# Moving the D*u term of a state-space scan from VectorE to ScalarE and TensorE, in twenty of its groups

## The chip, the cores and the metric

The kernel runs on one core of one Trainium2 chip. Its time is the device time of one execution in microseconds (us); of several runs the median is given. TensorE is called PE here, VectorE DVE, ScalarE ACT, GpSimd POOL and SyncE SP, as in the profile.

## The reference

Two layers, each a Mamba mixer and a mixture-of-experts feed-forward block, on an input of 4 x 512 rows of 512 features. What matters here is the mixer. For each of 2 layers, 4 batches and 512 channels e it computes, over l = 0..511,

```python
delta = softplus(dt_proj @ dt_low + dt_b)              # [b, e, l]
state = state * exp(delta * A[e, n]) + delta * u * Bm[n]   # n = 0..15
y[e]  = sum over n of state[n] * Cm[n]
y     = y + D[e] * u                                   # the term in question
y     = y * silu(z)
x     = x + transpose(y)
```

`u` is the activated output of a short convolution, which depends on the context input alone, so both layers' scans can be run one behind the other. The feed-forward block of layer 0 (shared expert and eight routed ones) follows from its mixer, that of layer 1 from the second mixer.

## The kernel before, in words

**Stages.** A first stretch projects and convolves for all eight pairs of layer and batch (`projections`). Then `scan_stage` runs 32 groups g = 0..31: layer 0's four batches of four blocks of 128 channels, then layer 1's. A group has 16 steps, one for each state i; one tile is 128 channels x 512 positions, fp32. Beside the scans of groups 4 to 19 the shared expert of layer 0 is worked off in small pieces (class `Beside`, `Shared`), beside groups 21 to 31 the routed experts of layer 0. After all of it come the feed-forward blocks of layer 1 (`stage_ffn1`).

**Order.** Each engine's program is written out by hand: the loop `steps()` gives (g, i), and each engine issues its instructions for this step and then `side.step(...)`, its pieces of the other work. An engine runs its queue in order; semaphores join the engines. For step (g, i), s = 16 g + i:

- ACT, L570: H[i % 4] = exp(delta * A), into one of four PSUM banks. It waits until hC of step s - 4 is done, which read that bank.
- POOL, L608: dBu[i % 2] = du * B[i]. It waits until scan s - 2 is done.
- DVE, L661: the scan of step s, in place in H. Then, for the step before, L641: hC = H * C, into a ring of SBUF buffers. In groups 0 to 19 the ring has three buffers (`ring`), so hC(i) waits until PE has added up hC(i - 3).
- PE, L511 (`add_up`): YS += ident x hC, in PSUM bank 4. In the trace an fp32 matmul is two records, here and elsewhere.

From group 20 on (`paired`) POOL adds some of the hC in pairs (L620), and the ring has four buffers.

**The bank YS** is used in turn. The sum of group g - 1 is complete after its add_up 15. DVE's `dve_y` (L646) at step `y_at[g]` of group g (1 in groups up to 19, 2 after) computes Y = Y * D + YS; Y held u until then. Then PE's dt_proj for group g + 1 (L499, step `y_at[g] + 1`) writes its product over YS, once `y_done` allows. ACT reads that product in `prep(g + 1, 0)` (L548, L549), which releases `pre_read`; `prep` goes on in three more steps with softplus's exp, square, logarithm and a linear term (L552 to L560), one part behind each exp of steps `y_at[g] + 3` to `y_at[g] + 6`. PE's first add_up of group g (`add_up(g, 0)`, issued at step `y_at[g] + 2` with those of v = 1 and 2) waits for that `pre_read`. POOL finishes delta for group g + 1: `pool_poly` (L583) at step 9, `pool_delta` (L587) at 13, `pool_du` (L593) at 14; DVE picks at step 11 (L625).

**Side work on DVE that the prediction names:** L1001 (norm of a row tile), L986 and L990 (the two halves of the gated product, the second after PE's up-projection), L981 (adds the down-projection of a tile to X), L945 (gate). PE's products for it are L1024, its transposes L1020 and L1038; on ACT L1085 and L1097 read them.

Of the kernel before, what the change touches and what calls it, by code (L numbers as in the profile page):

```python
# [30 lines left out]
B, L, D = 4, 512, 512  # L31
# [71 lines left out]
def program(nc, x, ctxT, mix, moe0, moe1, out):  # L103
    ctx = ExitStack()
    with ctx:
# [288 lines left out]
        def scan_stage(side):  # L394
# [12 lines left out]
            hC = [wk(6), wk(7), wk(8), wk(19)]  # L407
            side.y_done = y_done

            def paired(g):  # L410

                return g >= side.PAIRS
# [82 lines left out]
            def tensor(pe):  # L495
                def dt_proj(g):
                    if g == GROUPS // 2:
                        pe.wait_ge(dt1_in, 32)
                    nc.tensor.matmul(YS[:, :], dtwT[:, g % NJ * P:(g % NJ + 1) * P], xds[:, g // NJ % B, :],  # L499
                                     start=True, stop=True).then_inc(dt_done, 1)  # L500

                def add_up(g, v):
                    u = units[g][v]
                    if v == 0:
                        at_least(pe, y_done, g)
                        pe.wait_ge(pre_read, min(g + 2, GROUPS))
                    if len(u) == 2:
                        pe.wait_ge(pool_added, pairs0[g] + pairs[g].index(u) + 1)
                    else:
                        pe.wait_ge(hC_done, g * NS + u[0] + 1)  # L510
                    nc.tensor.matmul(YS[:, :], ident[:, :], hC[ring(g * NS + u[0])], start=v == 0,  # L511
                                     stop=v == len(units[g]) - 1).then_inc(sum_done, 1)

                def first_step(pe):
                    free(pe, "pe")
                    dt_proj(0)

                proj_pe(pe, first_step)
                side.before("pe", pe)
                for g, i, vb, n in steps():  # L520
                    if g:
                        for v in range(len(units[g - 1])):
                            if when(g - 1, v) == NS + i:
                                add_up(g - 1, v)
                    if i == y_at[g] + 1 and g < GROUPS - 1:
                        at_least(pe, y_done, g)
                        pe.wait_ge(pre_read, g + 1)
                        dt_proj(g + 1)
                    if i >= y_at[g] + 2:
                        for v in range(len(units[g])):  # L530
                            if when(g, v) == i:
                                add_up(g, v)
                    side.step("pe", pe, vb, n)
                for v in range(len(units[-1])):
                    if when(GROUPS - 1, v) >= NS:
                        add_up(GROUPS - 1, v)
                side.after("pe", pe)

            def scalar(act):
                def prep(g, step):  # L540

                    j, k = g % NJ, g // NJ // B
                    if step == 0:
                        act.wait_ge(dt_done, g + 1)
                        at_least(act, dA_done, (g - 1) * NS)
                        at_least(act, dBu_done, (g - 1) * NS)
                        at_least(act, delta_done, g)
                        nc.scalar.activation(delta[j % 2], YS[:, :], ACT.Relu, bias=dtb[k][:, j:j + 1])  # L548
                        nc.scalar.activation(logp, YS[:, :], ACT.Abs, bias=dtb[k][:, j:j + 1]).then_inc(pre_read, 1)  # L549
                    if step == 1:  # L550
                        act.wait_ge(pre_read, g + 1)
                        nc.scalar.activation(expo, logp, ACT.Exp, scale=-1.0).then_inc(t_done, 1)  # L552
                    if step == 2:
                        act.wait_ge(t_done, g + 1)
                        nc.scalar.activation(poly, expo, ACT.Square, bias=pbias[:, 0:1], scale=3.0 ** -0.5).then_inc(sq_done, 1)
                        nc.scalar.activation(du[j % 2], expo, ACT.Relu, bias=pbias[:, 1:2], scale=-1.0)
                    if step == 3:
                        nc.scalar.activation(logp, expo, ACT.Ln, bias=1.0)
                        act.wait_ge(sq_done, g + 1)
                        nc.scalar.activation(poly, poly, ACT.Identity, bias=pbias[:, 2:3]).then_inc(sp_l, 1)  # L560

                proj_act(act, lambda step: prep(0, step))
                free(act, "act")
                side.before("act", act)
                for g, i, vb, n in steps():
                    s = g * NS + i
                    if i == 0:
                        act.wait_ge(delta_done, g + 1)
                    at_least(act, hC_done, s - 3)
                    nc.scalar.activation(H[i % 4][:, :], delta[g % 2], ACT.Exp,  # L570
                                         scale=An[vb // B][:, g % NJ, i:i + 1]).then_inc(dA_done, 1)
                    if y_at[g] + 3 <= i <= y_at[g] + 6 and g < GROUPS - 1:
                        prep(g + 1, i - y_at[g] - 3)
                    if g == 1 and i == 0:
                        free(act, "act gates")
                    if vb <= B:
                        side.gate("act", act, vb, *divmod(n, NS))
                    side.step("act", act, vb, n)
                side.after("act", act)
# [69 lines left out]
            def vector(dve):  # L649
                def first_step(dve):  # L650
                    dve.wait_ge(poly_done, 1)
                    dve_pick(0)

                proj_dve(dve, first_step)
                stats(dve)
                side.before("dve", dve)
                for g, i, vb, n in steps():
                    s = g * NS + i
                    dve.wait_ge(dA_done, s + 1)
                    dve.wait_ge(dBu_done, s + 1)  # L660
                    nc.vector.tensor_tensor_scan(H[i % 4][:, :], H[i % 4][:, :], dBu[i % 2], 0.0,  # L661
                                                 ALU.mult, ALU.add).then_inc(scan_done, 1)
                    if s:
                        dve_hC(dve, s - 1)
                    if i == y_at[g] and g:
                        dve_y(dve, g - 1)
                    if i == 11 and g < GROUPS - 1:
                        dve.wait_ge(poly_done, g + 2)
                        dve_pick(g + 1)
                    side.step("dve", dve, vb, n)  # L670
                dve_hC(dve, GROUPS * NS - 1)
                dve_y(dve, GROUPS - 1)
                side.after("dve", dve)
# [1138 lines left out]
```

## Time and profile before

| | |
|---|---|
| time, median of 3 runs | 2232.88 us (2231.13 to 2234.89) |
| the profiled execution | 2236.41 us, its span 2234.6 us |
| PE, busy | 1926.2 us, 86% of the span |
| DVE, busy | 1397.7 us, 63% |
| POOL, busy | 1052.3 us, 47% |
| ACT, busy | 850.3 us, 38% |
| scans, L661 | 512 of 1222 ns, from 138.0 us to 1357.0 us |
| L646 | 32 of 736 ns, from 172.8 us to 1361.4 us |

The profile is of one execution. Busy shares are means over stages that differ; which engine holds up a stage is read from the groups of that stage, and from what its busiest engine waited for. A wait is put down to what came last. Group 0 begins at 138.0 us, group 20 at 893.9 us, group 21 at 944.6 us. Within a timeline each line is one instruction or a few like ones, with its start, its length, and, in brackets, the time for which its engine stood idle before it and who ended that.

### The profile page before, as it was taken

How to read it: one execution, taken by the hardware profiler on the slowest of the kernel's cores; microseconds unless marked ns; L12 is line 12 of the kernel's file. 1: busy time of each engine (PE TensorE's matmuls, PEld its weight loads, DVE VectorE, ACT ScalarE, POOL GpSimd, SP SyncE). 2: the span in 40 equal slices, each digit the busy share in tenths (PEclk: the TensorE clock that was granted, in tenths of full speed). 3: DMA queues.
4: the chain of work that ended last, by engine and by line, in shares of the span. 5: the costliest groups of instructions: out<-in, count | busy, mean ns of one | idle time of the engine just before them, and what ended most of it. 6: DMA issues, size and time to landing. Idle time of an engine off the chain costs nothing. (4 is left out here: it accounts for less than half of the span.)

```text
span 2234.6 us, 18612 instructions
## 1 busy us (share of the span) xinstructions
PE 1926.2 (86%) x5075; PEld 879.4 (39%) x5075; DVE 1397.7 (63%) x1934; ACT 850.3 (38%) x1372; POOL 1052.3 (47%) x927
## 2 busy tenths in 40 slices
PE   8846778789688796589999994999999999999997
PEld 2212233334233242134444442545455555555553
DVE  6899999899888988688888886564311111111100
ACT  4746545546464543555555551111011111111111
POOL 0057776676676664887777774110651110111111
PEclk9968799899899997589999997899999999999999
DMA  5099300302302102558769666212656665666554
GB/s 195 27 308 193 151 10 10 150 15 78 120 13 118 48 10 113 183 217 319 267 222 354 235 217 215 82 57 86 208 166 181 177 185 165 171 185 173 183 160 149
DMA packets 102625, 341.62 MB, mean 153 GB/s; under 512 B 16944, under 2 KB 17968, under 8 KB 84480
## 3 DMA queue, kind: packets, MB, share of 16 engines
q1 hardware_dynamic: 89008, 312.09, 40.8%
q0 software_dynamic: 13520, 28.40, 5.7%
q8 instruction: 41, 0.67, 0.1%
q14 instruction: 56, 0.46, 0.1%
HBM read 276.53 MB, written 65.74 MB: 153 GB/s over the span
## 5 line engine op out<-in xcount | busy, mean ns | idle before, releaser
L608 POOL TENSOR_TENSOR work<-work,big 128x512 f32<-128x512 f32 x512 | 653.9, 1283 | 232.3 <-DVE bank L661 231.1
L511 PE MATMUL bank<-work,ident 128*128 128x512 f32 x928 | 533.3, 688 | 206.5 <-DVE work L641 156.6
L661 DVE TENSOR_TENSOR_SCAN bank<-bank,work 128x512 f32<-128x512 f32 x512 | 625.4, 1222 | 95.4 <-POOL work L608 50.9
L570 ACT ACTIVATE bank<-work,An 128x512 f32<-128x512 f32 x512 | 347.6, 690 | 324.8 <-DVE work L641 323.4
L511 PEld LDWEIGHTS bank<-work,ident 128*128 128x128 f32 x928 | 173.6, 210 | 509.8 <-DVE work L641 330.5
L641 DVE TENSOR_TENSOR work<-bank,big 128x512 f32<-128x512 f32 x512 | 344.8, 674 | 7.9 <-PE bank L511 7.5
L1723 PE MATMUL bank<-Y,big 128*128 128x512 f32 x528 | 259.2, 595 | 0.0
L1561 POOL DMA_INDIRECT out_rows<-Y,meta x39 | 61.3, 1571 | 375.8 <-ACT Y L1235 271.6
L1258 DVE SCALAR_TENSOR_TENSOR work<-work,bank 128x352 f32<-128x352 f32 (+1 forms) x62 | 35.9, 579 | 302.3 <-ACT work L1248 302.3
L1024 PE MATMUL bank<-W,work 128*128 128x512 f32 x384 | 191.6, 603 | 0.0
L1737 PE MATMUL bank<-big,W 128*128 128x512 f32 x352 | 168.3, 593 | 0.0
L1235 ACT ACTIVATE Y<-bank,meta 128x512 f32<-128x512 f32 x39 | 26.8, 687 | 293.7 <-PE bank L1213 278.8
L1723 PEld LDWEIGHTS bank<-Y,big 128*128 128x128 f32 x528 | 99.0, 191 | 82.6 <-issue 57.0
L1213 PE MATMUL bank<-work 128*128 128x512 f32 (+1 forms) x234 | 114.3, 600 | 4.1 <-DMA work<-down_last 4.1
L1202 PE MATMUL bank<-work 128*128 128x352 f32 x312 | 110.7, 460 | 1.3 <-DMA work<-up 1.3
L1263 DVE SCALAR_TENSOR_TENSOR work<-work,bank 128x352 f32<-128x352 f32 (+1 forms) x62 | 35.9, 579 | 120.9 <-PE bank L1202 120.9
L1674 ACT ACTIVATE work<-bank 128x512 f32<-128x512 f32 x44 | 26.2, 597 | 222.1 <-PE bank L1723 222.1
L1192 PE MATMUL bank<-work 128*128 128x352 f32 x312 | 105.9, 464 | 1.3 <-DMA work<-gate 1.3
L1024 PEld LDWEIGHTS bank<-W,work 128*128 128x128 f32 x384 | 72.6, 193 | 84.3 <-issue 84.2
L583 POOL TENSOR_TENSOR work<-work 128x512 f32<-128x512 f32 x32 | 40.6, 1268 | 115.0 <-ACT work L560 115.0
L1737 PEld LDWEIGHTS bank<-big,W 128*128 128x128 f32 x352 | 65.3, 190 | 58.6 <-issue 46.0
L1622 DVE SCALAR_TENSOR_TENSOR W<-work,bank 128x512 f32<-128x512 f32 x44 | 30.2, 686 | 92.7 <-PE bank L1723 92.4
(258 smaller groups left out, 2373.1 us busy)
## 6 DMA issues: line engine op xcount, KB each, us to landing
big<-bc_d SPq DMA_DIRECT2D x64, 1024.0 KB, 6.6
work<-gate SPq DMA_DIRECT2D x39, 704.0 KB, 4.2
work<-up SPq DMA_DIRECT2D x39, 704.0 KB, 4.2
W<-gate SPq DMA_DIRECT2D x23, 1024.0 KB, 4.9
W<-up SPq DMA_DIRECT2D x23, 1024.0 KB, 5.5
W<-down SPq DMA_DIRECT2D x23, 1024.0 KB, 5.3
work<-down SPq DMA_DIRECT2D x39, 512.0 KB, 3.7
work<-xs_d SPq DMA_DIRECT2D x62, 256.0 KB, 4.8
```

The lines of the kernel that those rows point to most:

```text
L511: nc.tensor.matmul(YS[:, :], ident[:, :], hC[ring(g * NS + u[0])], start=v == 0, stop=v == len(units[g]) - 1).then_inc(sum_done, 1)
L570: nc.scalar.activation(H[i % 4][:, :], delta[g % 2], ACT.Exp, scale=An[vb // B][:, g % NJ, i:i + 1]).then_inc(dA_done, 1)
L608: nc.gpsimd.tensor_tensor(dBu[i % 2], du[g % 2], Bb[:, i, :], ALU.mult).then_inc(dBu_done, 1)
L641: nc.vector.tensor_tensor(hC[ring(s)], H[i % 4][:, :], Cb[:, i, :], ALU.mult).then_inc(hC_done, 1)
L661: nc.vector.tensor_tensor_scan(H[i % 4][:, :], H[i % 4][:, :], dBu[i % 2], 0.0, ALU.mult, ALU.add).then_inc(scan_done, 1)
L1024: ins = nc.tensor.matmul(dst[:, :], at[:, c * P:(c + 1) * P], w[:, c, :], start=c == 0, stop=c == DK - 1)
L1192: ins = nc.tensor.matmul(self.G[:, 0:self.F], self.xT[q][:, c * P:(c + 1) * P], self.wg[:, c, :], start=c == 0, stop=c == DK - 1)
L1202: ins = nc.tensor.matmul(self.U[:, 0:self.F], self.xT[q][:, c * P:(c + 1) * P], self.wu[:, c, :], start=c == 0, stop=c == DK - 1)
L1213: ins = nc.tensor.matmul(self.TB[:, :], self.hT[0:fn, c * P:(c + 1) * P], self.wd[0:fn, c, :], start=c == 0, stop=c == len(self.chunks) - 1)
L1561: nc.gpsimd.indirect_dma_start(out=out, out_offset=bass.IndirectOffsetOnAxis(ap=meta[:, t, 0:1].bitcast(U32), axis=0), in_=ex.yo[t % 2], i ...
L1723: ins = nc.tensor.matmul(dst[:, :], sgu[:, c, u // DK * FS + f * P:u // DK * FS + (f + 1) * P], xTb[b][:, c, :], start=c == 0, stop=c == D ...
L1737: ins = nc.tensor.matmul(down_bank(b, r)[:, :], hT[c][:, r * P:(r + 1) * P], sdw[:, c, :], start=c == 0, stop=c == NF - 1)
```

## The change

For groups 0 to 19 (`by_pe`; `side.PAIRS` is 20) the term D*u goes another way. At step 11 of group g, ACT scales Y (which holds u) by D in place. PE adds ident x Y into YS right before the last add_up of the group, behind the wait for its hC. At step 4 of the next group, behind exp(4), ACT copies YS to Y, which now releases `y_done`; `dve_y` is left out. Where that copy is made, `prep(g + 1, ...)` stands behind the exps of steps 6 to 9, not 4 to 7 (in group 20: 6 to 9, not 5 to 8). PE's dt_proj and add_ups stay at their steps.

```diff
+            u_scaled = sem("s_u_scaled")
+            def by_pe(g):
+                return 0 <= g < side.PAIRS
@@ add_up
                         pe.wait_ge(hC_done, g * NS + u[0] + 1)
+                    if by_pe(g) and v == len(units[g]) - 1:
+                        pe.wait_ge(u_scaled, g + 1)
+                        nc.tensor.matmul(YS[:, :], ident[:, :], Y[:, g % (B * NJ), :], start=False, stop=False)
                     nc.tensor.matmul(YS[:, :], ident[:, :], hC[ring(g * NS + u[0])], start=v == 0,
                                      stop=v == len(units[g]) - 1).then_inc(sum_done, 1)
@@ scalar
-                    if y_at[g] + 3 <= i <= y_at[g] + 6 and g < GROUPS - 1:
-                        prep(g + 1, i - y_at[g] - 3)
+                    if i == 4 and by_pe(g - 1):
+                        act.wait_ge(sum_done, sums0[g])
+                        nc.scalar.copy(Y[:, (g - 1) % (B * NJ), :], YS[:, :]).then_inc(y_done, 1)
+                    if i == 11 and by_pe(g):
+                        act.wait_ge(du_done, g + 1)
+                        nc.scalar.activation(Y[:, g % (B * NJ), :], Y[:, g % (B * NJ), :], ACT.Copy,
+                                             scale=dsk[g // NJ // B][:, g % NJ:g % NJ + 1]).then_inc(u_scaled, 1)
+                    first = 6 if by_pe(g - 1) else y_at[g] + 3
+                    if first <= i <= first + 3 and g < GROUPS - 1:
+                        prep(g + 1, i - first)
@@ vector
-                    if i == y_at[g] and g:
+                    if i == y_at[g] and g and not by_pe(g - 1):
                         dve_y(dve, g - 1)
```

## Rows read from the trace of the kernel before

**Rows 1.** The page: busy tenths of PE and DVE in 40 equal slices of the span.

```profile
PE   8846778789688796589999994999999999999997
...
DVE  6899999899888988688888886564311111111100
```

**Rows 2.** Busy time by stretch: groups 2, 8, 10 and 18; columns in the first line.

```profile
core 0: us, PE busy (x) PEld busy (x) DVE busy (x) ACT busy (x) POOL busy (x), PEclk, DMA share, GB/s
...
201.60:233.80 32.20, 21.57 (x34) 6.05 (x34) 31.19 (x37) 18.66 (x27) 25.00 (x21) 0.85 0.53 113
...
420.60:456.60 36.00, 23.78 (x50) 8.91 (x51) 34.44 (x45) 16.65 (x24) 25.74 (x22) 0.80 0.16 66
495.00:533.60 38.60, 34.63 (x99) 16.03 (x100) 36.22 (x45) 20.96 (x31) 25.89 (x23) 1.00 0.02 8
...
804.10:845.50 41.40, 41.06 (x118) 19.61 (x117) 35.69 (x48) 18.52 (x29) 25.80 (x22) 1.00 0.02 7
```

**Rows 3.** DVE's waits from 138 to 894 us: us in total, times, longest.

```profile
DVE bank L661 <- POOL work L608: 25.8, 17, 2.7
DVE X L981 <- PE bank L1024: 16.8, 5, 4.6
DVE bank L661 <- ACT bank L570: 6.5, 10, 1.0
DVE Y L646 <- PE bank L511: 6.3, 9, 2.3
DVE work L990 <- PE bank L1024: 3.5, 3, 1.7
DVE work L641 <- PE bank L511: 3.5, 4, 1.1
```

**Rows 4.** Timeline, start of group 2: start us, length us, engine, line, operation.

```profile
203.41 1.12 PE L511 MATMUL bank<-work,ident 128*128 128x512 f32 x2 [0.59 <-DVE work L641]
204.40 0.67 DVE L641 TENSOR_TENSOR work<-bank,big 128x512 f32<-128x512 f32 x1
...
204.99 0.73 DVE L646 SCALAR_TENSOR_TENSOR Y<-Y,dsk,bank 128x512 f32<-128x512 f32 x1
205.11 0.69 ACT L570 ACTIVATE bank<-work,An 128x512 f32<-128x512 f32 x1 [1.03 <-DVE work L641]
205.64 1.23 DVE L661 TENSOR_TENSOR_SCAN bank<-bank,work 128x512 f32<-128x512 f32 x1
...
206.94 0.69 ACT L548 ACTIVATE work<-bank,dtb 128x512 f32<-128x512 f32 x1 [1.14 <-PE bank L499]
...
207.53 0.68 ACT L549 ACTIVATE work<-bank,dtb 128x512 f32<-128x512 f32 x1
...
208.31 2.38 PE L511 MATMUL bank<-work,ident 128*128 128x512 f32 x5 [1.40 <-issue]
208.49 0.67 DVE L641 TENSOR_TENSOR work<-bank,big 128x512 f32<-128x512 f32 x1
...
210.21 0.67 DVE L641 TENSOR_TENSOR work<-bank,big 128x512 f32<-128x512 f32 x1
```

**Rows 5.** Timeline, start of group 8: the first add_ups and hC(3).

```profile
428.86 2.90 PE L511 MATMUL bank<-work,ident 128*128 128x512 f32 x3 [1.40 <-issue]
...
431.01 0.69 DVE L641 TENSOR_TENSOR work<-bank,big 128x512 f32<-128x512 f32 x1 [1.11 <-PE bank L511]
```

**Rows 6.** Timeline, DVE: scan 8 of group 2, and norm in group 9.

```profile
217.04 1.23 DVE L661 TENSOR_TENSOR_SCAN bank<-bank,work 128x512 f32<-128x512 f32 x1 [1.01 <-ACT bank L570]
...
466.21 1.14 DVE L1001 TENSOR_SCALAR work<-X,mvr,rstd 128x512 f32<-128x512 f32 x1
```

**Rows 7.** Timeline, start of group 10: PE's products, L646 and L990.

```profile
499.14 1.88 PE L1024 MATMUL bank<-W,work 128*128 128x512 f32 x4
...
499.34 0.75 DVE L646 SCALAR_TENSOR_TENSOR Y<-Y,dsk,bank 128x512 f32<-128x512 f32 x1 [0.80 <-PE bank L511]
...
502.33 0.68 DVE L990 SCALAR_TENSOR_TENSOR work<-work,bank 128x512 f32<-128x512 f32 x1
```

**Rows 8.** One line's instructions, L1085: duration min/median/max in ns.

```profile
L1085 ACT COPY work<-bank x16: 560/578/585, 302.7 to 816.7; 128x512 f32<-128x512 f32 x16
```

## The prediction

> **What bounds the kernel now.** I read the 40 slices first [rows 1]. The scans run from slice 3 to slice 25; from there to about slice 16 the DVE row stands at 8 or 9 and PE at 6 to 9. In the last 17 slices DVE is nearly out of it and PE is at 9, but the change touches nothing there. Next come single groups [rows 2]: in 32.2 us of group 2, DVE is busy 31.2 us and PE only 21.6; in group 10 DVE 36.2 and PE 34.6 of 38.6; in group 18 PE 41.1 of 41.4. The granted clock is 1.00 in the last two, 0.85 and 0.80 in groups 2 and 8. So groups 0 to 19 are DVE's, with PE close behind in the groups that carry much of the feed-forward work, and ahead of it in group 18. Then what DVE waited for in that stretch [rows 3]: 25.8 us for dBu of POOL, 16.8 us for products of PE before L981, 6.5 us for exp of ScalarE, 6.3 us before its y step L646, 3.5 us before L990 and 3.5 us before the product with C, L641. That is 63 us of some 750, so an instruction taken from DVE should be worth its own length, unless it leaves a wait behind. Groups 20 to 31 and the second layer come after the stretch in series, so what is won or lost in it reaches the end whole.
>
> **The loop that matters.** One group boundary, in order of time, is the core of the argument [rows 4]. YS is one PSUM bank with three users in turn: the state sum of group g-1, the delta projection of group g+1 (L499), and the state sum of group g, whose first term add_up(g, 0) may overwrite the bank only when prep(g+1) step 0 (L548, L549) has read it (`pre_read`). And hC is a ring of three buffers: hC(3) of group g writes over hC(0), so it waits for that add_up. The rows show the whole loop in group 2. DVE's hC(0) ends at 205.07; L646 runs from 204.99 to 205.72 beside exp(4) at 205.11; then L499; ScalarE reads the bank from 206.94 to 208.21; add_up(0) starts at 208.31; hC(3) starts at 210.21, and has waited for nothing: some 0.8 us of slack. In group 8, with PE at 1.2 GHz, the same hC(3) does wait, 1.11 us for L511 [rows 5].
>
> **What is removed.** Twenty L646 steps, the ones for groups 0 to 19. L646 starts at 204.99 and the scan behind it at 205.64 [rows 4]: 0.65 us each, 13.0 us. The 6.3 us of waits before them go as well [rows 3]. Together -19.3 us.
>
> **What is moved, and its price.** ScalarE's prep(g+1) moves from step 4 to step 6. It stands there behind exp(6), and exp(6) needs H[2], so it waits for hC(2) of the same group; before, step 0 stood behind exp(4), which needs only hC(0). Now nothing between hC(2) and hC(3) can run ahead of time. From hC(2)'s end to hC(3)'s start, at full clock [rows 4]: 0.04 us to exp(6) (as 205.07 to 205.11); exp 0.69 less the 0.10 by which two ScalarE instructions overlap (L548 starts at 206.94, lasts 0.69, L549 starts at 207.53), 0.59; L548 to L549 0.59; L549 0.68; 0.10 to PE (208.21 to 208.31); one add_up of two records 1.12; 0.04 to DVE. Sum 3.16 us. DVE itself needs from hC(2)'s end (208.49 + 0.67 = 209.16) to 210.21, 1.05 us, in which it runs the next scan. So DVE stands 2.1 us at hC(3), once in each of groups 1 to 19 (group 20 has a ring of four and is held by POOL): 19 x 2.1 = +40 us. This is the largest term, and the new wait is longer than the step that it replaces. Behind the waiting add_up(0) all of PE's queue stands, the products of the feed-forward among it.
>
> **What takes some of it away.** In the four groups with g % 4 == 1, norm (L1001, 1.14 us) lies on DVE between hC(2) and the next scan [rows 6]: 4 x 1.1 = -4.4 us. The 3.5 us that hC already waits for L511 are part of the same wait: -3.5 us. In six groups (1, 2, 3, 7, 11, 15) the scan of step 8 waits 0.9 to 1.0 us for exp(8), stuck behind prep; [rows 6] have group 2's, 1.01 us, the longest. Two steps later, with DVE held at hC(3), ScalarE has the time: -5.7 us.
>
> **What PE's extra work adds.** ident x Y is one more add_up, two records, 0.86 us of PE at full clock (four records of L1024 take 1.88 us with the last one's tail [rows 7], 0.43 apart); 20 of them are 17 us of PE. Where PE has gaps they cost nothing. But they stand at the group boundary, ahead of products that DVE's side work needs. In group 10 DVE waits 0.80 us at L646, and L990 starts at 502.33 [rows 7]; the products that it needs end at 501.02 and will end at 501.88. Without L646 and its wait DVE is 1.45 us earlier, but L990 can start only 0.4 us earlier: 1.05 us of the gain comes back as a wait for PE. I take the same for the eight groups with g % 4 of 2 or 3: +8.4 us.
>
> **The new ScalarE work.** A copy of YS, 0.58 us by the nearest row, L1085 [rows 8], behind exp(4), and a scaling of Y at step 11, no longer than an exp, 0.69 us. Both lie in time in which ScalarE waits for DVE; in [rows 4] it idles from 205.80 to 206.94. They are costed at nothing; if that cover were gone it would be 20 x 1.3 = 25 us. The copy's end comes about 0.7 us after L646's did, and PE's L499 with it; that too is hidden, since prep now waits for exp(6) anyway.
>
> **The clock.** In group 2, PE waited 1.40 us before add_up(0) [rows 4]; with prep at step 6 it waits about 3. In group 8 the first add_ups run at 1.2 GHz, and from 428.86 to hC(3) at 431.01 pass 2.15 us instead of 1.16 [rows 5]. PE's load is low in groups 1 to 4, 8, 12 and 16 (two of them in [rows 2]). I take 1.0 us more for each: +7 us, with none and twenty as bounds. TensorE: Matmul & The Clock Gate of the Trainium skill (What's actually happening) says that throttling is the default and that recent activity releases it; group 8's rows agree. By that rule every group whose PE now stands idle before add_up(0) would meet the low clock, not only the seven; that is the third rival below.
>
> **The rest.** Group 18 is PE's own [rows 2], so there the blocked queue (about 1.9 us) and one more add_up count in full, 1.3 us beyond what DVE's term has. In group 19 and at group 20's start PE's products come one more add_up late, by my estimate 0.86 us each. Together +3 us.
>
> **Sum:** -19.3 + 40 - 4.4 - 3.5 - 5.7 + 8.4 + 7 + 3 = +25.5, say +26 us. The profiled execution took 2236.4 us, 1.8 more than its span; that gives 2262.4. The median of the runs is 3.5 us below the profiled one, so I forecast 2259 us, 1.2% slower. Bounds: with no return of PE's waits and no low clock, +8 to +10 us (2241 to 2243); with the low clock in all groups, +13 more (2272), and with L499 and the added term at low clock too, some +20 (2279).
>
> **Rivals.**
> 1. The gain arrives and no new wait comes: hC(3) has its slack and ScalarE its lead. -19.3 us, 2214 us. For it: ScalarE idles much in these groups, and DVE is the bound. Against it: ScalarE's queue keeps its order, exp(6) cannot start before hC(2) ends, and the rest of the loop is longer than one scan. It decides if the loop from hC(2) to hC(3) were under 1.05 + 0.65 us; its rows make 3.16. Chance 0.04.
> 2. It comes out even: PE's extra work and the late wait take just what DVE gives, within 0.2% (4.5 us, about what a measurement of this kernel can tell from no change). It needs at least five of the 40 us hidden by side work beside the low bound. Near 2233 us. Chance 0.03.
> 3. The slow side, further out: PE's added idle time drops its clock in nearly all groups, so add_up(0), L499 and the extra term run at 1.2 GHz and DVE's later waits for L1024 grow. 2272 to 2279 us. For it: group 8 shows the low clock already with a wait of 1.40 us. Against it: groups 6, 7, 10 and 11 keep PE fed, 34.6 of 38.6 us in group 10. Chance 0.15.
> 4. The change does not do what it says: L646 stays in groups 20 to 31, and is gone elsewhere, which the diff leaves no doubt of. Under 0.01.
> The forecast itself: 0.77, within 2241 to 2272. The range, 2241 to 2278, takes in most of rival 3. Faster 0.05, same 0.03, slower 0.92.
>
> **What the profile after would show.** L646 twelve times instead of 32. DVE's wait at L641 for PE's L511 up from 3.5 us to some 45, once a group before the same product. On ScalarE, L548 directly behind an exp that was released by L641, with no wait for L499. PE's L511 with 40 more records, and its wait before add_up(0) ended by ScalarE's L549. The waits for exp at step 8 gone. The length of group 2 up from 32.2 us to about 33.5, and of group 8 from 36.0 to 37.6; groups 21 and on unchanged. The forecast is wrong if hC(3) starts within 1.5 us of hC(2)'s end, if the step-8 wait returns at step 10 in place of vanishing (POOL's poly step waits for prep's end there), or if the later part does not keep the shift.

## The result and the profile after

Four runs of the changed kernel give a median of 2263.89 us (2260.3 to 2264.76), four of the kernel before 2233.89 us. The ratio is 1.0132 (95% interval 1.0118 to 1.0146): slower, by 30 us in the medians. The profiled execution took 2260.3 us, its span 2258.5 us; beside the span of before, 2234.6 us, that is 24 us. The 2259 us that were forecast lie 5 us below the median, inside the range.

The line numbers have moved: scan L661 is now L678, hC L641 is L658, exp L570 is L579, add_up L511 is L520, prep's L548 and L549 are L557 and L558, dt_proj L499 is L505, the pick L625 is L642, the gate L945 is L962, L981 is L998, L990 is L1007, the feed-forward's L1024 is L1041. The added term's product is L519, the copy L583.

The 40 slices of the page, PE and DVE, beside [rows 1]: in the scans' slices they are hardly to be told apart, and PE is busy for 86% of the span in both. What the change costs doesn't show in busy shares.

```profile
PE   8856678779788787569999995899989999999997
...
DVE  6898898888889888788888886654410111111100
```

DVE's waits from 137.6 to 918.9 us, groups 0 to 19, beside [rows 3]: us in total, times, longest.

```profile
DVE work L658 <- PE bank L520: 46.6, 26, 3.0
DVE bank L678 <- POOL work L625: 29.4, 26, 2.7
DVE X L998 <- PE bank L1041: 13.4, 5, 2.9
DVE work L1007 <- PE bank L1041: 9.3, 7, 2.1
DVE bank L678 <- ACT bank L579: 4.8, 7, 1.5
```

The line of L646, 6.3 us, is gone. The line of hC, L658, has gone from 3.5 to 46.6 us and heads the list; 43.8 us of it are hC(3) in groups 1 to 19, once in each.

Busy time by stretch, groups 2, 8, 10 and 18, beside [rows 2]: DVE's busy time is less in groups 2, 10 and 18 (29.21 us in group 2, not 31.19) and 0.5 us more in group 8, and all four are longer: 33.3, 38.5, 40.5 and 44.1 us.

```profile
202.80:236.10 33.30, 24.26 (x36) 7.50 (x36) 29.21 (x36) 20.04 (x29) 25.41 (x21) 0.80 0.46 99
426.00:464.50 38.50, 25.68 (x53) 9.97 (x54) 34.92 (x43) 18.06 (x26) 25.58 (x22) 0.80 0.16 61
504.50:545.00 40.50, 35.74 (x101) 16.33 (x102) 35.81 (x44) 22.43 (x33) 25.94 (x23) 1.00 0.02 7
820.60:864.70 44.10, 42.20 (x119) 19.71 (x119) 34.85 (x45) 20.02 (x31) 25.74 (x22) 1.00 0.02 7
```

The loop itself, beside [rows 4]: timeline of group 2 from hC(2) to hC(3), start and length in us.

```profile
209.47 0.67 DVE L658 TENSOR_TENSOR work<-bank,big 128x512 f32<-128x512 f32 x1
...
210.06 1.22 DVE L678 TENSOR_TENSOR_SCAN bank<-bank,work 128x512 f32<-128x512 f32 x1
210.18 0.69 ACT L579 ACTIVATE bank<-work,An 128x512 f32<-128x512 f32 x1 [0.29 <-DVE work L658]
210.81 0.67 ACT L557 ACTIVATE work<-bank,dtb 128x512 f32<-128x512 f32 x1
...
211.38 0.68 ACT L558 ACTIVATE work<-bank,dtb 128x512 f32<-128x512 f32 x1
...
212.15 4.11 PE L520 MATMUL bank<-work,ident 128*128 128x512 f32 x6 [2.73 <-issue]
...
213.35 0.69 DVE L658 TENSOR_TENSOR work<-bank,big 128x512 f32<-128x512 f32 x1 [2.08 <-PE bank L520]
```

hC(2) ends at 210.14, exp(6) follows 0.04 later, the two readers of the bank behind it, add_up(0) at 212.15, hC(3) at 213.35: 3.21 us, where it was 1.05, and 2.08 us of them idle DVE. In group 8 the same chain passes through a slow add_up, beside [rows 5]:

```profile
435.58 3.98 PE L520 MATMUL bank<-work,ident 128*128 128x512 f32 x5 [1.77 <-issue]
437.73 0.69 DVE L658 TENSOR_TENSOR work<-bank,big 128x512 f32<-128x512 f32 x1 [3.02 <-PE bank L520]
```

From add_up(0) to hC(3) it takes 2.15 us, not 1.20; the wait is 3.02 us. That is so in groups 1, 3, 4, 8, 12, 16 and 19; the waits are 2.08 us in groups 2, 6, 7, 10, 11, 14, 15 and 17, 1.08 in 5, 9 and 13 (norm lies beside), 2.77 in 18.

Added up over groups 0 to 20 from the start of their scans, the scans take 26.0 us more. Groups 21 to 27 don't differ, groups 28 to 30 give 2.5 us back. That is not the change's doing: every other trace, also those of the kernel before with a small edit, has these groups 1.3 to 2.8 us shorter than the one trace of before.

### The profile page after: what moved, and what is told of

It reads as the page before. It is cut to its first block and busy times, and to the rows that moved or that the text cites. A ratio compares the mean times of both kernels' runs of the same rounds, so it can differ in the third digit from the quotient of the medians.

```text
span 2258.5 us, 18732 instructions
## 1 busy us (share of the span) xinstructions
PE 1938.7 (86%) x5115; PEld 887.5 (39%) x5115; DVE 1379.1 (61%) x1914; ACT 876.7 (39%) x1412; POOL 1055.9 (47%) x927
## 5 line engine op out<-in xcount | busy, mean ns | idle before, releaser
L625 POOL TENSOR_TENSOR work<-work,big 128x512 f32<-128x512 f32 x512 | 655.5, 1287 | 236.7 <-DVE bank L678 235.3
L520 PE MATMUL bank<-work,ident 128*128 128x512 f32 x928 | 525.6, 680 | 202.9 <-DVE work L658 125.6
L678 DVE TENSOR_TENSOR_SCAN bank<-bank,work 128x512 f32<-128x512 f32 x512 | 625.1, 1221 | 96.7 <-POOL work L625 53.1
L579 ACT ACTIVATE bank<-work,An 128x512 f32<-128x512 f32 x512 | 347.4, 690 | 350.5 <-DVE work L658 349.4
L658 DVE TENSOR_TENSOR work<-bank,big 128x512 f32<-128x512 f32 x512 | 344.6, 673 | 52.3 <-PE bank L520 51.4
L520 PEld LDWEIGHTS bank<-work,ident 128*128 128x128 f32 x928 | 176.7, 210 | 498.2 <-DVE work L658 262.1
L1041 PE MATMUL bank<-W,work 128*128 128x512 f32 x384 | 188.8, 595 | 0.0
L1041 PEld LDWEIGHTS bank<-W,work 128*128 128x128 f32 x384 | 71.3, 190 | 81.8 <-issue 81.7
L1209 PE MATMUL bank<-W,work 128*128 128x512 f32 x184 | 87.3, 606 | 0.7 <-ACT work L1238 0.7
```

The costliest lines, as they stand in the source:

```text
L625: nc.gpsimd.tensor_tensor(dBu[i % 2], du[g % 2], Bb[:, i, :], ALU.mult).then_inc(dBu_done, 1)
L658: nc.vector.tensor_tensor(hC[ring(s)], H[i % 4][:, :], Cb[:, i, :], ALU.mult).then_inc(hC_done, 1)
L1041: ins = nc.tensor.matmul(dst[:, :], at[:, c * P:(c + 1) * P], w[:, c, :], start=c == 0, stop=c == DK - 1)
L1209: ins = nc.tensor.matmul(self.G[:, 0:self.F], self.xT[q][:, c * P:(c + 1) * P], self.wg[:, c, :], start=c == 0, stop=c == DK - 1)
```

## The experiments

Times are medians; but for one kernel that was run once, the ratio to the kernel before, run on the same chip beside it (2232.7 to 2233.9 us), stands with its 95% interval. Two theories were to be told apart: the time is lost in the loop hC(2), exp(6), prep, add_up(0), hC(3); or it is lost to the new work on ScalarE and TensorE.

### The move of prep alone, in the kernel before

```diff
-                    if y_at[g] + 3 <= i <= y_at[g] + 6 and g < GROUPS - 1:
-                        prep(g + 1, i - y_at[g] - 3)
+                    first = 6 if 1 <= g <= side.PAIRS else y_at[g] + 3
+                    if first <= i <= first + 3 and g < GROUPS - 1:
+                        prep(g + 1, i - first)
```

> The kernel before, with one part of the change alone: prep(g+1) stands behind the exps of steps 6 to 9 in groups 1 to 20; D*u stays on DVE as it was, no new copy, no new PE term. Theory A (the moved bank read closes a loop from hC(2) over exp(6), L548, L549 and add_up(0) to hC(3)): DVE waits at hC(3) once in each of groups 1 to 19, 2.1 us with PE at full clock and 3.0 us at half clock, some 44 us in all as in the changed kernel; less what the changed kernel also gained by the late prep (waits for exp, shorter picks and gates, shorter wait before the last row addition), some 18 us: 2252 to 2262 us. Rival B (the time went to PE's twenty extra terms and ScalarE's forty extra instructions, and the place of prep costs nothing): within 0.2% of before, 2230 to 2238 us.

Measured: 2281.11 us, 1.0216 (1.0199 to 1.0233). With none of the new work, and L646 still on DVE, the kernel is 48 us slower: more than with the whole change. DVE's waits in it, 137.6 to 942 us:

```profile
DVE work L642 <- PE bank L511: 50.5, 19, 3.0
DVE bank L662 <- POOL work L609: 27.8, 22, 2.7
DVE X L982 <- PE bank L1025: 12.1, 6, 2.9
DVE work L991 <- PE bank L1025: 9.8, 4, 4.2
```

The loop is the cause, and the size expected of it was some 20 us or more short. hC(3)'s wait grows from 3.5 to 50.5 us, 47.0 us in one line. It is longer than in the changed kernel (43.8) since 14 groups, not 7, now have all or most of add_up(0) at the low clock. In group 2 PE has stood still for 4.27 us before it, not 2.73:

```profile
213.46 3.74 PE L511 MATMUL bank<-work,ident 128*128 128x512 f32 x4 [4.27 <-issue]
...
215.61 0.69 DVE L642 TENSOR_TENSOR work<-bank,big 128x512 f32<-128x512 f32 x1 [3.03 <-PE bank L511]
```

The longer standstill comes from dt_proj. Here it runs right behind L646, 3.4 us before hC(2) ends; in the changed kernel it waits for the copy and starts 1.8 us before that. The product that is missing at the group's end plays a part too; the run without it, below, gives its share.

### Prep one and two steps earlier, with and without the change

In the changed kernel, one step:

```diff
-                    first = 6 if by_pe(g - 1) else y_at[g] + 3
+                    first = 5 if by_pe(g - 1) else y_at[g] + 3
```

> The changed kernel with prep(g+1) behind the exps of steps 5 to 8, not 6 to 9, in groups 1 to 20. Theory A: L548 then starts when exp(5) is through or PE's projection has landed, 0.7 to 1.1 us before hC(2) ends where it started 0.66 us after it, so the wait at hC(3) falls from 2.1 to about 0.8 us (groups 6 and 10 to about 0.4), 1.3 to 1.7 us a group, some 25 us; some 3 us of waits for exp come back: 2238 to 2246 us. Rival B (PE's and ScalarE's added work): no change, 2260 to 2265 us.

In the kernel before, the edit of the first experiment with one line changed:

```diff
-                    first = 6 if 1 <= g <= side.PAIRS else y_at[g] + 3
+                    first = 5 if 1 <= g <= side.PAIRS else y_at[g] + 3
```

> The kernel before with prep(g+1) alone moved by one step, behind the exps of steps 5 to 8, in groups 1 to 20. Theory A: L548 starts about 1.1 us before hC(2) ends, the scan's product hC(3) waits 0.3 us with PE at full clock and 1.3 us at half clock, 6 to 15 us in all, against some 6 us of waits for exp(8) and a few slow picks that go: 2233 to 2243 us, a small part of the 48 us that two steps cost. With the changed kernel at the same steps at 2233.6 us this also prices D*u's move by itself with prep at one place. Rival B (the place of prep is not what costs, and the two-step kernel was slow for another reason): no ordering by steps, anything outside 2230 to 2250 us.

In the changed kernel, two steps:

```diff
-                    first = 6 if by_pe(g - 1) else y_at[g] + 3
+                    first = 4 if by_pe(g - 1) and g < side.PAIRS else y_at[g] + 3
```

> The changed kernel with prep(g+1) at its old steps 4 to 7, right behind the new copy. Theory A: ScalarE stands before L548 for the copy, L505 and their hand-overs, so L548 starts no earlier than with steps 5 to 8 where PE is slow, and about 0.6 us earlier where PE is quick; exp(5) is held up behind it. The wait at hC(3) is at or below that of steps 5 to 8, the waits for exp at step 8 are back at 0.9 us or more in ten groups or so: 2236 to 2248 us. Rival B: no change, 2260 to 2265 us.

| D*u on | prep at steps 4 to 7 | 5 to 8 | 6 to 9 |
|---|---|---|---|
| DVE | 2232.88 (before) | 2230.11, 0.999 (0.9978 to 1.0002) | 2281.11, 1.0216 (1.0199 to 1.0233) |
| ScalarE and TensorE | 2238.45, 1.0025 (1.0015 to 1.0035) | 2233.58, 1.0004 (0.9994 to 1.0014) | 2263.89, 1.0132 (1.0118 to 1.0146) |

Read along a line: the step from 5 to 6 costs 51 or 30 us, that from 4 to 5 gives 3 or 5 (the 3 lies within the noise). Behind exp(5) the loop starts at hC(1), one scan and one hC (1.72 us) earlier. The hC(3) wait in group 2 of the changed kernel with prep at step 5:

```profile
208.31 0.69 DVE L658 TENSOR_TENSOR work<-bank,big 128x512 f32<-128x512 f32 x1 [0.46 <-PE bank L520]
```

0.46 us instead of 2.08. Summed over groups 1 to 19 it is 13.9 us instead of 43.8, and the kernel came out better than the 2238 to 2246 us that were expected of it. In the kernel before with prep at step 5 it is 8.9 us, in the seven groups with a low clock or near it, at most 1.31 each. With prep at step 4 hC(3) waits no less, 13.9 us: ScalarE is held by dt_proj there (1.22 us in group 2), which now starts behind the copy. But exp(8) comes 1.5 to 1.7 us late in groups 2, 3, 7, 11 and 15, and in groups 0 to 20 DVE's waits for ScalarE make 13.4 us (7.0 with prep at step 5).

That kernel came within the 2236 to 2248 us expected of it. The kernel before with prep at step 5 came out 3 us better than its 2233 to 2243.

Read down a column: the moved term costs 5.6 us with prep at 4 and 3.5 us with prep at 5 (there the intervals overlap), and gives 17 us back with prep at 6. In that last column DVE's hC(3) waits 50.5 us without it and 43.8 with it. These 6.7 of the 17 us are a matter of TensorE's clock at add_up(0). The rest is about what the moved L646 (13 us) and its waits (4.8 us in the kernel with prep moved alone) took, less what the product costs PE.

### The term's product left out

```diff
-                        nc.tensor.matmul(YS[:, :], ident[:, :], Y[:, g % (B * NJ), :], start=False, stop=False)
```

> The changed kernel without PE's twenty products ident x Y; the term D*u is left out of the output of groups 0 to 19, all waits stay. Theory A: PE's extra 0.86 us a group counts only where DVE's side work waits for PE behind it (L1007 and L998 in groups with g % 4 of 2 or 3, and groups 17 to 19), about 8 us: 2253 to 2259 us, with the 44 us of waits at hC(3) unchanged. Rival B: the twenty terms cost their full 17 us and the state sum's later end more, 2245 us or less.

This kernel leaves D*u out of the output of groups 0 to 19. Measured: 2251.94 us, 1.009 (1.0066 to 1.0114). By the medians the product costs the changed kernel 12 us, by the two profiled spans 7.8 us; some 8 were expected. The four runs spread over 10 us, so these can't be told apart. The wait of L1006 (L1007 in the changed kernel) falls from 9.3 to 5.1 us:

```profile
DVE work L657 <- PE bank L519: 46.8, 19, 3.0
...
DVE work L1006 <- PE bank L1040: 5.1, 5, 2.1
```

The hC waits stay (46.8 us), and all of them are now hC(3): 43.8 us of it with the product, 3.0 us more without. Groups 2, 5, 9 and 13 now have add_up(0) at the low clock too and wait 0.94 us longer each, group 18 waits 0.7 us less. So the clock that the product holds up is 3 to 4 of the 6.7 us above, by one trace of each kernel. The rest are mainly groups 10, 11, 14 and 15, slow only in the kernel with prep moved alone; the earlier dt_proj there is the likely reason, which no run shows by itself. Groups 16, 18 and 20 are 2.6, 0.7 and 0.6 us shorter. Of the 30 us some 8 to 12 hang on PE's added product; the loop remains without it.

### The copy made twice

```diff
+                        nc.scalar.copy(expo, YS[:, :])
                         nc.scalar.copy(Y[:, (g - 1) % (B * NJ), :], YS[:, :]).then_inc(y_done, 1)
```

> The changed kernel with ScalarE's new copy of YS made twice at step 4 (the first into the buffer expo, free then), 0.58 to 0.61 us more in each of groups 1 to 20. Theory A: L548 stands behind exp(6), which waits for hC(2), so the second copy lies in ScalarE's idle time and the hC(3) waits stay; only where PE's projection L505 was late already (group 18, and 8 and 12 at half clock) it shows: 0 to 3 us, 2263 to 2268 us. Rival C (ScalarE's extra instructions are on the path): 12 us more, 2275 us.

Measured: 2266.13 us, 1.0153 (1.0135 to 1.017), 2.2 us over the changed kernel, for twenty more copies of 0.59 us; the intervals overlap. ScalarE's work at step 4 is hidden, as the prediction had it, except where PE is full: hC(3) of group 18 waits 4.6 us in this kernel, 2.77 in the changed one. The rival, that the copy is on the path and costs its full length, falls. The scaling at step 11 was not tried by itself.

### TensorE kept at work before the first add_up

```diff
+                        if 1 <= g <= 4:
+                            for _ in range(2):
+                                nc.tensor.matmul(bank[7][:, :], ident[:, :], xds[:, 0, :], start=True, stop=True)
```

> The changed kernel with two products added on PE right behind L505 in groups 1 to 4, into a bank nobody uses then (the same output; 1.7 us of PE at full clock in each), where PE stood idle 3.0 us before add_up(0). Theory A with the clock part: PE's idle time before add_up(0) falls to about 1.3 us, the granted clock stays at 2.4 GHz in more of these groups, and the wait at hC(3), 3.0 us in groups 1, 3 and 4 and 2.1 in group 2, is 2.1 us in all four: up to 3 us less in all. Rival D (the 3.0 us have another cause than the clock): the waits stay at 3.0 us.

Measured: 2259.24 us, one run. Group 2's loop was at the high clock already; in groups 1, 3 and 4 add_up(0)'s first record goes from 1191 to 667 ns, and hC(3) waits 2.08 us in all four groups. Groups 8, 12 and 16, which were not fed, still wait 3.03. The 0.94 us between the two kinds of groups is TensorE's clock: it is granted at 1.2 GHz during add_up(0) in the one kind and at 2.4 GHz in the other. Work on PE just before helps to hold it up, but it isn't all that decides. In this trace groups 13, 14 and 17, which were not fed, fell to the low clock for all or most of add_up(0), with nearly the same idle time before it as in the changed kernel's trace (2.69, 1.06 and 2.37 us), where they kept the high one. So hC(3) waits 44.4 us over groups 1 to 19, no less than the 43.8 before; the feeding shows in its four groups and not in the sum. Rows of group 2 in this kernel, the last three records of the idle products and then 1.01 us of idleness, not 2.73:

```profile
208.72 1.45 PE L540 MATMUL bank<-xds,ident 128*128 128x512 f32 x3
...
211.18 4.79 PE L520 MATMUL bank<-work,ident 128*128 128x512 f32 x10 [1.01 <-issue]
...
212.38 0.69 DVE L661 TENSOR_TENSOR work<-bank,big 128x512 f32<-128x512 f32 x1 [2.08 <-PE bank L520]
```

### The change in sixteen groups

Groups 16 to 19 are 14.7 us longer in the changed kernel than before; PE is busy for 83% of group 17 there and 96% of group 18. So the term stays on DVE there, and prep stands at step 5. First with the term's product ahead of add_up 13:

```diff
-                return 0 <= g < side.PAIRS
+                return 0 <= g < 16
-                    if by_pe(g) and v == len(units[g]) - 1:
+                    if by_pe(g) and v == 13:
-                    first = 6 if by_pe(g - 1) else y_at[g] + 3
+                    first = 5 if by_pe(g - 1) else y_at[g] + 3
```

> D*u by ScalarE and PE in groups 0 to 15 only (sixteen, not twenty), prep at steps 5 to 8 behind those, and the product ident x Y issued two add_ups earlier, before that of hC(13). With prep at 5 to 8 and all twenty groups, groups 1 to 16 came out 9.6 us shorter than before and groups 17 to 20 6.2 us longer, PE being full there. Theory A: the 9.6 us stay and the 6.2 us go: 2219 to 2228 us. Rival B: no difference to before, 2233 us.

Measured: 2233.12 us, 1.0004 (0.9996 to 1.0013). A miss: nothing of the gain came. With the product two steps earlier PE does less in the last steps ahead of the boundary. In this trace the low clock meets add_up(0) in groups 2 to 4, 8, 12 and 16, and dt_proj as well in 8, 12, 16 and, in part, 3:

```profile
423.37 2.08 PE L505 MATMUL bank<-xds,dtwT 128*128 128x512 f32 x2 [1.15 <-ACT Y L583]
...
429.00 0.69 DVE L658 TENSOR_TENSOR work<-bank,big 128x512 f32<-128x512 f32 x1 [2.35 <-PE bank L520]
```

Then the same with the product back ahead of the last add_up:

```diff
-                    if by_pe(g) and v == 13:
+                    if by_pe(g) and v == len(units[g]) - 1:
```

> D*u by ScalarE and PE in groups 0 to 15, prep at steps 5 to 8 behind those, the product ident x Y again before the last add_up; only this place differs from the kernel that came out level with the kernel before. There, groups 3, 8, 12 and 16 had waits of 2.1 to 2.4 us at hC(3) with PE at half clock, where the kernel with twenty groups and the late product had 0.5 to 1.7. Theory A: the late product keeps PE at work at the group boundary; groups 1 to 16 come out some 9 us shorter than before, 17 to 20 as before: 2220 to 2228 us. Rival B: within 0.2% of before, the place of the product is without effect and the clock falls by chance of phase.

Measured: 2223.43 us, 0.9959 (0.9946 to 0.9972). hC(3) waits 0.46 us in groups 1 to 4 and 1.16 in group 8, where it was 2.35; where the product stands is worth 10 us. Of these, 6 lie in hC(3)'s waits (17.8 against 11.7 us over groups 1 to 19). Groups 17 to 19, 11.2 us longer in the changed kernel than before, are now as before within 0.2 us.

Last, idle products into a free bank in the groups with little work for PE:

```diff
+                    if g in (1, 2, 3, 4, 8, 12, 16) and (i == 2 or i >= 5 and (g < 4 or i < 7)):
+                        nc.tensor.matmul(bank[7][:, :], ident[:, :], xds[:, 0, :], start=True, stop=True)
```

> The kernel with sixteen groups and the late product, and on PE one more product without use (into a bank idle then; the same output) at step 2 and at steps 5 to 15 of groups 1 to 3, and at steps 2, 5 and 6 of groups 4, 8, 12 and 16. Theory A with the clock part: PE stays at 2.4 GHz in these seven groups, the hC(3) waits there are 0.5 to 0.8 us, 3 to 6 us less than without: 2217 to 2225 us. Rival D (feeding PE costs its own time, since the queue is in order and the products stand before add_up(0)): the same or slower than without, 2225 us or more.

Measured: 2218.86 us, 0.9938 (0.9925 to 0.995), 14 us faster than before and 4.6 us faster than without the idle products. DVE's waits up to 905 us:

```profile
DVE bank L680 <- POOL work L627: 31.4, 23, 2.7
DVE work L660 <- PE bank L520: 14.3, 19, 1.7
DVE X L1000 <- PE bank L1043: 12.0, 5, 2.9
```

The timeline at hC(3) of group 8:

```profile
419.68 0.69 DVE L660 TENSOR_TENSOR work<-bank,big 128x512 f32<-128x512 f32 x1 [0.46 <-PE bank L520]
```

hC(3) waits 0.46 us in all of groups 1 to 4, 8, 12 and 16. Groups 0 to 20 are 16.9 us shorter than before. So the idea of the change carries, once the loop is short, PE has room for the product, and its clock is held. What was not tried is the same idle products in the kernel before, where hC(3) waits 3.5 us for an add_up(0) at the low clock: a part of the last 4.6 us may be had without moving D*u.

### The pick ahead of the product with C

The trace showed something that no step of the prediction had (below): the pick at step 11 takes 0.72 us or up to 1.69. In the kernel before it was moved ahead of the hC of step 10, right behind scan 11:

```diff
+                    if i == 11 and g < GROUPS - 1:
+                        dve.wait_ge(poly_done, g + 2)
+                        dve_pick(g + 1)
...
-                    if i == 11 and g < GROUPS - 1:
-                        dve.wait_ge(poly_done, g + 2)
-                        dve_pick(g + 1)
```

> The kernel before with one swap on DVE: at step 11 the pick (copy_predicated, L625) is issued right behind the scan, ahead of hC(10), not behind it. In the changed kernel six picks fell from 1.69 to 0.72 us; all fast ones began when POOL's running operation had little left. Theory P (DVE's instructions with two SBUF inputs stand still while a POOL operation that began earlier runs): right behind the scan POOL's dBu has not begun, so the picks of groups 0 to 19 take 0.72 us where 14 of them took 1.4 to 1.7, some 0.9 us each, and dBu is delayed in their place by less than its slack or little more: 2220 to 2228 us. Rival Q (the slow picks have another cause, or the time comes back as waits for dBu): picks still at 1.4 us or more, or 2231 to 2237 us.

Measured: 2226.48 us, 0.9973 (0.9964 to 0.9983). The picks of groups 0 to 19 take 17.8 us instead of 25.3 (half of them 0.71 to 0.74 us, half 1.03 to 1.05, where all were expected at 0.72), and the kernel is 6 to 7 us faster. Last, this edit in the sixteen-group kernel with the idle products:

> e12 (sixteen groups, preparation at steps 5 to 8, the term ahead of the last add_up, idle products that hold TensorE's clock; 2218.86 us against 2233) with the pick issued between scan 11 and the hC of step 10, as in e13, which alone took some 6 us off the kernel before. Theory (pick's length goes by whether POOL's operation has begun before it, and that has nothing to do with the add_up loop): the two gains stand in different steps of a group and add: 2218.9 - 6 to 8, so 2209 to 2215 us; picks of groups 1, 2, 3, 7, 11, 15 at 0.72 to 1.05 us. Rival (in the kernel with the term on ScalarE and TensorE the picks of these groups are already short, 0.72 us, since DVE reaches them at another time than POOL; the earlier issue then only moves the wait ahead of scan 12 or the norm): no gain, 2217 to 2221 us. Second rival (hC of step 10 comes later, bank free later, the add_up loop feels it at the half clock): slower than e12, 2221 to 2227 us.

Measured: 2217.55 us, 0.9934 (0.9922 to 0.9947). Expected were 2209 to 2215 us. The gains don't add: 1.3 us under the kernel without it, and the intervals lie over each other. The time of the rival came, but not for its reason. The picks were long there and did become short; the time went to other places. Forms of DVE work up to 905 us, total us and mean ns, first without the edit, then with it:

```profile
L644 DVE COPY_PREDICATED work<-work 128x512 f32<-128x512 uint32 x20 | 25.4, 1269 | 0.0
L1020 DVE TENSOR_SCALAR work<-X,mvr,rstd 128x512 f32<-128x512 f32 x16 | 15.0, 940 | 0.0
```

```profile
L1020 DVE TENSOR_SCALAR work<-X,mvr,rstd 128x512 f32<-128x512 f32 x16 | 19.4, 1210 | 0.0
...
L644 DVE COPY_PREDICATED work<-work 128x512 f32<-128x512 uint32 x20 | 17.8, 888 | 0.0
```

The picks give 7.6 us, the norms take 4.4 of them, in groups 4, 8, 12 and 16, where each is 1.0 to 1.1 us longer; the waits of DVE grow by 3.8 us. The likely reading is that DVE's longer steps and POOL's keep step with each other through the whole group, so that shifting one shifts which pair collides.

## Why the prediction was right or wrong

Right in direction and in the main cause; the size came as near as it did in part by luck. By its own steps, the terms as the traces give them, waits for groups 0 to 19 where nothing else is said:

| step | worked out | measured |
|---|---|---|
| L646 and its waits gone | -19.3 | -13.2 and -6.3: -19.5 |
| hC(3), net of what it waited before, with norm and the low clock | 40 - 4.4 - 3.5 + 7 = +39.1 | 43.8 - 3.5 = +40.3 |
| late exp(8) gone | -5.7 | 6.5 to 4.8: -1.7; group 20 adds +2.3 |
| products of PE come late | +8.4 | L1007 +5.8, L998 -3.4: +2.4 |
| full PE in groups 18 to 20 | +3, with the other terms +7.7 for groups 17 to 20 | groups 17 to 20 are +11.8 in all |
| waits for POOL | nothing | +3.6, with group 20 +1.6 |
| picks and gates | nothing | -5.7 and -5.0 |

The sum was +25.5 us. The spans differ by 23.9, and groups 0 to 20, which the terms are about, by 26.0. The last groups' line is no term of its own: it holds their share of the other lines. Without it and with group 20 the measured column makes +14.7. The other 11 us are things that the prediction did not have: 3.7 us of waits of other hC for PE, 2.6 us more in the hC steps themselves, 2.0 us in the routing's small operations, 1.2 us of waits at L977 (it adds to a row tile of X), 0.9 us in norm, and smaller ones. That the sum came so near is in part luck. Short picks and gates (-10.7 us) and PE's return (6 us less than its term) stand on one side, these 11 us, the exps (6 us more than their term) and waits for POOL on the other.

**The loop** was right in each link. 3.16 us were worked out from hC(2)'s end to hC(3)'s start, 3.21 are measured. The first experiment shows that the move of prep alone makes it; the two with prep at step 5, that one step of slack removes most of it. The norm was taken for four groups; it lies between hC(2) and the next scan in three (5, 9 and 13), and takes 1.0 us off the wait there. In group 17 it comes one step earlier, and hC(3) waits the full 2.08 us.

**The low clock** was put at 1.0 us in seven groups; it is 0.94 in seven, but group 2 is not among them and group 19 is. The rival that all groups fall to the low clock did not happen in the changed kernel. With prep moved alone it came nearest to happening, in 14 groups. The rule of the Trainium skill that it leaned on (TensorE: Matmul & The Clock Gate, What's actually happening: throttled unless recent activity releases the clock) agrees in kind with the fed groups 1 to 4. By idle time before add_up(0) alone the groups can't be told apart: it is 2.73 us in group 2, at 2.4 GHz, and 2.72 in group 16, at 1.2.

**The late exp at step 8** was half wrong, and the prediction had named the sign of it. It is gone in groups 7, 11 and 15, but came back at step 10 in groups 1 to 3 (0.84 us each) and is new in group 18 (1.51 us). Timeline of group 2 in the changed kernel:

```profile
218.86 1.28 ACT L567 ACT_TABLE_LOAD   x1
...
220.16 0.63 ACT L567 ACTIVATE work<-work 128x512 f32<-128x512 f32 x1
...
221.41 1.28 ACT L579 ACT_TABLE_LOAD   x1
...
222.71 1.30 ACT L579 ACTIVATE bank<-work,An 128x512 f32<-128x512 f32 x2
...
224.07 1.23 DVE L678 TENSOR_TENSOR_SCAN bank<-bank,work 128x512 f32<-128x512 f32 x1 [0.84 <-ACT bank L579]
```

The logarithm in prep's last part costs ScalarE two table loads of 1.28 us, there and back. That part now stands behind exp(9), so exp(10) is late. The error was to reckon only what DVE's hold at hC(3) gives ScalarE, not that the dear part of prep comes four steps after it, when the lead is spent.

**PE's return to L990** was worked out for group 10 and then multiplied by eight. In group 10 it is exact: the wait is 1.02 us, 1.05 was worked out, beside [rows 7]:

```profile
511.50 0.69 DVE L1007 SCALAR_TENSOR_TENSOR work<-work,bank 128x512 f32<-128x512 f32 x1 [1.02 <-PE bank L1041]
```

Groups 6 and 14 have the same; in the kernel without the product these three waits are 0.27 us. In groups 7, 11 and 15 it didn't come; instead L998 waits 2.9 us, not 4.4 to 4.6: DVE reaches it later, PE is done at its own time. One group was taken for eight that differ.

**The last groups** were put too low: by the prediction's terms groups 17 to 20 cost 7.7 us more (three times 2.1 for the loop, -1.1 for norm, two times 1.05 for L990, +3, less four L646), and they took 11.8. The hC(3) part (2.08, 2.77 and 3.02 us) is as foreseen but for the low clock in group 19. Beyond it stand exps that come 3.5 us later in groups 18 and 20, and in group 19 a wait at L998 that is 1.5 us longer and the routing's small operations on DVE, which take 5.2 us, not 3.2. That these were longer is seen; why is not settled. Nor is a full PE the main reason. Without the added product these groups are still 10.1 us longer than before, and with prep moved alone, in the kernel before, 15.0. With prep at step 5 and the term moved in all twenty groups, 6.2 us remain. The sixteen-group kernels, where groups 17 to 20 have prep and term as before, are back at the old time there.

**The new ScalarE work at nothing** holds for the copy: twenty further ones cost 2.2 us, with intervals that overlap. For the scaling at step 11 no run shows it by itself.

**The span and the median.** The profiled run of after was the lowest of its four; the medians differ by 30 us, the profiled pair by 24. The forecast had set the median 3.5 us under the profiled time, as it was for before; for after it is 3.6 us above.

## What to carry to other kernels

Taking a step off the busiest engine is worth nothing until the new place of what was moved behind it is followed link by link: draw the loop through every in-order queue, from the buffer that is waited for to the instruction that frees it, and count the steps of slack. One step of a queue was worth 30 to 50 us here, the whole moved operation 3 to 17. Where a kernel's busy engine hands work to one that idles at its boundaries, look at that engine's load and clock group by group, and move the work only where it has both.

## What was not expected of the hardware

**DVE and POOL get in each other's way on SBUF, and who comes first waits least.** Pick and POOL's operation beside it in group 2, before and after:

```profile
223.84 2.48 POOL L608 TENSOR_TENSOR work<-work,big 128x512 f32<-128x512 f32 x2
...
225.24 1.67 DVE L625 COPY_PREDICATED work<-work 128x512 f32<-128x512 uint32 x1
```

```profile
226.37 2.96 POOL L625 TENSOR_TENSOR work<-work,big 128x512 f32<-128x512 f32 x2
...
227.52 0.72 DVE L642 COPY_PREDICATED work<-work 128x512 f32<-128x512 uint32 x1
```

Before, POOL's second product had begun 0.18 us ahead of the pick, and the pick took 1.67 us. After, the first of the two had begun 1.15 us ahead and was nearly done; the pick took 0.72 us and ended 0.60 us after it, and it is POOL's pair that is stretched, 2.96 us instead of 2.48. Over groups 1 to 19 of before, whenever a product of POOL had begun first (by 0.18 to 0.43 us), the pick ended 0.59 to 0.61 us after that product's end; where the pick came first, by 0.35 to 0.37 us, it took 0.73 or 0.74 us and POOL's product 1.46 to 1.48 instead of 1.27. hC, with one input in PSUM, takes 0.67 us beside POOL or not. The Trainium skill (SBUF — State Buffer, Who interferes with whom) says that a DVE instruction with two SBUF inputs and a GpSimd instruction that reads SBUF share a port pair by an exclusive lock, and that whoever issues first keeps it for the whole instruction. These rows agree.

**Where a product stands matters as much as that it stands.** With the added term ahead of the last add_up the clock stays up through the boundaries of groups 1 to 4; with it two steps earlier only that of group 1 is spared, and the kernel is 10 us slower. The clock part is seen in one trace of each kernel. The 48 idle products of the last sixteen-group kernel cost no time that shows, and lift the mean clock of the span from 0.939 to 0.950.
